# One added wait: an expert's weights are loaded once a scatter has landed

## The reference

```python
scores = softmax(xf @ gate_w.T); topk_w, topk_idx = top_k(scores, 6)      # 64 experts
# each expert takes at most CAP = 128 tokens, in order
buf_tok, buf_w = ...                     # (64, 128): token numbers (T where empty) and weights
gx = xp[buf_tok]                         # gather of 128 rows for each expert
g, u = split(einsum('ech,ehi->eci', gx, gate_up_proj))                    # 512 -> 2 x 192
eo = einsum('eci,eih->ech', silu(g) * u, down_proj) * buf_w[..., None]    # 192 -> 512
routed = zeros.at[buf_tok].add(eo)       # scatter-add
shared = silu(xf @ shared_gate_w.T) * (xf @ shared_up_w.T) @ shared_down_w.T
x = x + routed + shared
```

## Time and profile before

| | us |
|---|---|
| median of 3 runs | 767.88 |
| lowest, highest | 761.12, 768.71 |
| profiled execution, its own time | 772.35 |
| its span in the trace | 770.6 |
| mean granted TensorE clock | 0.903 of full |

### The profile page before, as it was taken

How to read it: one execution, slowest core, us unless ns; L and a number is a source line. 1 busy time by engine, 2 the same in 40 slices (tenths; PEclk the granted TensorE clock), 3 DMA queues, 4 the chain that set the end, 5 groups by cost and what they waited for, 6 DMA issues and landing times.

```text
span 770.6 us, 5725 instructions
## 1 busy us (share of the span) xinstructions
PE 603.0 (78%) x1787; PEld 305.2 (40%) x1787; DVE 304.1 (39%) x724; ACT 144.9 (19%) x298; POOL 223.0 (29%) x191
## 2 busy tenths in 40 slices
PE   5989840498999999988877787897788787977770
PEld 2434320244444444544443344453444443534330
DVE  2987942566679882312212122212122222121120
ACT  4463430244400000111101111111011111110100
POOL 2135664000000003224324334423244433332422
PEclk9999965699999999998998899989898989898995
DMA  9817431731110134798987899878798989888933
GB/s 243 241 56 86 132 111 54 201 110 62 67 58 0 36 132 146 223 279 234 257 227 212 227 270 258 245 219 238 218 273 244 264 244 259 238 242 207 278 48 41
DMA packets 50757, 138.31 MB, mean 179 GB/s; under 512 B 11232, under 2 KB 13920, under 8 KB 50720
## 3 DMA queue, kind: packets, MB, share of 16 engines
q1 hardware_dynamic: 34464, 98.00, 41.2%
q0 software_dynamic: 16256, 39.87, 23.7%
HBM read 107.89 MB, written 29.89 MB: 179 GB/s over the span
## 4 chain that ended last, share of the span: by engine, by line
DMA 50%; PE 16%; issue 7%; DVE 6%; ACT 1%; POOL 0%; POOLq 0%; DVEq 0%; SPq 0%
DMA out<-y,table 50%; PE bank L852 6%; PE bank L864 3%; DVE val L1099 2%; DVE cand L1098 2%; PE bank L832 2%; PE bank L928 2%; PE bank L825 1%; PE bank L916 1%; ACT xnT L948 1%; DVE x L1094 0%; DVE shid L1089 0%; PE bank L908 0%; DMA both<-cand 0%; DVE krep L1070 0%
## 5 line engine op out<-in xcount | busy, mean ns | idle before, releaser
L794 POOL DMA_INDIRECT out<-y,table x64 | 101.6, 1587 | 287.6 <-DMA out<-y,table 259.3
L928 PE MATMUL bank<-gu_w,gxT 128*128 128x384 f32 x512 | 182.4, 501 | 1.2 <-ACT gxT L999 0.8
L1173 DVE TENSOR_SCALAR y<-bank,gx 128x512 f32<-128x512 f32 x64 | 48.1, 751 | 276.9 <-DMA out<-y,table 172.9
L916 PE MATMUL bank<-dn_w,hidT 96*128 96x512 f32 x256 | 145.5, 698 | 1.6 <-DVE hidT L1185 1.6
L928 PEld LDWEIGHTS bank<-gu_w,gxT 128*128 128x128 f32 x512 | 97.0, 200 | 55.6 <-issue 6.4
L800 POOL DMA_INDIRECT gx<-rows_dram,table x64 | 63.5, 992 | 159.1 <-DVE table L1164 139.9
L908 PE MATMUL bank<-ident,gx 128*128 128x128 f32 x256 | 44.9, 303 | 80.9 <-DMA gx<-rows_dram,table 80.9
L852 PE MATMUL bank<-xnT,upT 128*128 128x512 f32 x192 | 84.2, 595 | 0.0
L908 PEld LDWEIGHTS bank<-ident,gx 128*128 128x128 f32 x256 | 32.7, 153 | 109.5 <-DMA gx<-rows_dram,table 98.4
L1007 ACT ACTIVATE eg<-bank 128x192 f32<-128x192 f32 x64 | 21.2, 332 | 283.0 <-PE bank L928 283.0
L916 PEld LDWEIGHTS bank<-dn_w,hidT 96*128 96x128 f32 x256 | 50.7, 219 | 40.8 <-issue 38.3
(11 more groups left out here) (137 smaller groups left out, 456.2 us busy)
## 6 DMA issues: line engine op xcount, KB each, us to landing
gu_w<-in_gate_up SPq DMA_DIRECT2D x64, 768.0 KB, 5.8
dn_w<-in_down SPq DMA_DIRECT2D x64, 384.0 KB, 7.3
rows_dram<-rows SPq DMA_DIRECT2D x4, 1152.0 KB, 4.3
x<-in_x SPq DMA_DIRECT2D x4, 1024.0 KB, 8.5
feat_dram<-feat SPq DMA_DIRECT2D x4, 1024.0 KB, 5.2
out<-x SPq DMA_DIRECT2D x4, 1024.0 KB, 4.4
w<-in_W SPq DMA_DIRECT2D x5, 256.0 KB, 7.3
nodes<-in_ctx SPq DMA_DIRECT2D x4, 256.0 KB, 5.7
```

The lines of the kernel that those rows point to most:

```text
L794: pool.indirect_dma_start(a["out"][:, :], bass.IndirectOffsetOnAxis(ap=table[:, e:e + 1], axis=0), y[:, e % YB, :], None, compute_op=ALU.a ...
L916: last = nc.tensor.matmul(DN[:], hidT[:, e % 2, j, :], dn_w[:, e % U, j, :], start=(j == 0), stop=(j == 1))
L928: last = nc.tensor.matmul(GU[e % 2][:, 0:2 * I], gxT[:, e % 2, c, :], gu_w[:, e % U, c, :], start=(c == 0), stop=(c == KC - 1))
L1173: nc.vector.tensor_scalar(y[:, e % YB, :], DN[:], gx[:, e % GX, D + e:D + e + 1], None, ALU.mult).then_inc(y_ready, 1)
```

## The change

The loop of weight loads on SP's queue gets a second wait. The first (down of e-4 done, the buffer is free) stays. The added one waits until the scatter of expert e-4 has landed. As the diff's loop variable is the expert that is loaded, this is the scatter of expert e for the weights of e+4.

```diff
                 for e in range(U, E):
                     sp.wait_ge(dn_done, e - U + 1)
+                    sp.wait_ge(scat, 16 * (e - U + 1))
                     load_expert(sp, e, e % U)
```

## The result

The changed kernel has a median of 774.97 us over 20 runs (771.42 to 781.94); the kernel before, over its 20 runs, 769.58 (761.12 to 777.50). The ratio is 1.0098, with a 95% interval of 1.007 to 1.0127. I timed the change again in two more series, each beside the kernel before on one chip: 1.0049 (1.002 to 1.0078) and 1.0038 (1.0007 to 1.0068). So it loses 3 to 8 us. I had said 763.7 us, 0.5% less than before. The time lies in the range that I gave (750 to 780) and within the 1% that I called likeliest, but on the other side, and outside the 758 to 771 us of my first case. That case was for intervals of 7.03 to 7.25 us, and the intervals came out in it; what they add up to did not. I had scaled to a median of 767.88 from 3 runs, and 20 runs gave 769.58.

A forecast was written before the change was run, and what follows sets the result against it. The row of scatters, each waiting for the last to land, was taken as the bound. Terms of -6.2, -0.8, -1.8 and +4.6 summed to -4.2 us, giving 763.7 us on the median's scale; range 750 to 780.

The forecast's parts named there:

- my first case: The forecast proper: intervals between scatters of 7.03 to 7.25 us, time 758 to 771 us, chance 0.60.
- The middle: Scatter 5 to 58: 53 intervals at 7.13 us for 7.163, so 1.8 us less.
- four clean pairs: Four ask-and-scatter pairs in the old trace, ask 0.64 to 0.94 us before the scatter's issue; mean interval 7.13 us.
- The start: Scatter 0 to 5: the early burst of loads is spread out; 6.2 us less from scatter 1, 0.8 from scatter 0.
- Scatter 0: First scatter, with no load out: 5.63 us to the next issue for 6.38, so 0.8 us less.
- The end: Scatter 58 to 63: fewer scatters fly without a load beside them; 32.7 us for 28.1, 4.6 more.
- The place of the ask and of the loads: Each load asked for 0.69 us before a scatter's issue, both weights landed 5.97 us after the ask.
- A: Rival, scatters fly longer: ask falls after the issue, interval 7.93 for 7.13, 48 us in all, 812; chance 0.12.
- B: Rival, the load comes on the path: 7.67 us per scatter, +32 us, 796; chance 0.06.
- The slack of 3.2 us: Loop from landing through load, TensorE and VectorE takes 18.2 us for three scatters, where the scatters take 21.4.
- C: Rival, an even stream packs better: 6.9 us per interval, -14 us more, 750; chance 0.22.
- My floor of 6.3 us: The DMA engines' work per interval, taken from a busy share of 0.88; as an interval it would give 714 us.

The follow-up runs named there:

- marked_scatter: The change, but each load waits for a count that GpSimd raises by a memset behind the scatter, not for a landing: 697.94 us, ratio 0.9026.
- before_again: The kernel before the change, with no edit, timed and traced a second time: 771.57 us, ratio 1.0001.

## Why the prediction was wrong

**The middle: 7.13 us for an interval, which measured 7.21.** This is the term that turned the sign. Times 53 it is 4.2 us of the 5.7 us between the predicted -4.2 and the traces' +1.5. The price was the mean of four clean pairs, flight 6.34 plus 0.79. The three traces of the change have flights of 6.36 to 6.41 on average, which is 0.04 more and 2.3 us of the 4.2. My rows held that too: the four scatters landed 7.11 us after their loads' asks on average, with the ask 0.77 before the issue. I used their flight for an ask that I put at 0.69 before; the same landing makes 6.38 at the measured 0.73. The rest, 0.03, is not flight: in every trace of either kernel the interval after scatter 36 holds some 0.9 us in which GpSimd waits for nothing, the one after 52 some 0.3, and in two traces of the change scatter 24 waits for y. I set four pairs without such an event against the 7.163 of the earlier trace rows, which is a mean with the first two in it. A mean should have been compared with a mean: with these two events my pairs give 7.155, and a gain of 0.4 us in place of 1.8. That lucky and unlucky pairs "cancel to the same number" was said without a reason.

**The start: -7.0, measured -4.9.** The direction and the cause are right. Some 0.9 us of the miss is that the trace I read had the slowest start of the three: 34.7 us from scatter 1 to 5, for 33.0 and 33.9. Another 1.0 is that the four intervals took 29.0 to 30.2 us for my 28.5. They are 7.25 to 7.54 us each, longer than in the middle, and no run shows why. Scatter 0 gave 0.5 for the 0.8.

**The end: +4.6, measured +4.1.** Right.

**The place of the ask and of the loads.** I said 0.69 us before the issue; it is 0.73. I said 5.97 us from ask to landed; medians are 0.37 + 5.4 = 5.8. TensorE's wait for each load (some 2 us) is 1.6, the gathers' wait is gone, flights lie nearly all near 6.4. Scatter 5 was issued at 346.8 to 351.5 for my 347. These signs came nearly as written.

**Rivals.** A (flights grow by as much as the ask slips) was priced nearly right, at 7.93 for an ask 0.09 after the issue: 7.95 was measured at 0.14 before and 8.30 at 0.32 after. It did not happen in the change, whose ask does not slip. B (the load on the path) happened once in the first trace, at scatter 24, where SP took 1.23 us over one issue and `dn_w` landed after 6.7: the 5.1 us wait in the fence above. The slack of 3.2 us was nearly right: in the three traces of the change y(e) is done 3.3 us (median) before scatter e is issued, 3.1 with my allowance of 0.25 taken off. At scatter 24 it was 0.3 to 0.75 before that allowance. C (an even stream packs better) did not come from evenness, but it came, at ten per cent, once the even stream was shifted by 2.4 us. My floor of 6.3 us for an interval was no floor. It came from a busy share of 0.88 as if 1.00 were the most, but marked_scatter runs at 6.00 us with a share of 1.04. The packets' time per interval is the same in both, 1.04 x 6.00 and 0.87 x 7.17 (before_again), each 6.2 us: the work did not shrink, the gaps went.

**What stays open.** The traces account for +1.5 us (three each), the series measured +2.9, +3.8 and +7.5 us by their ratios. The first series remains higher than the traces explain.

## What to carry to other kernels

When two transfers share the DMA engines and only one of them is on the path, ask for the other so late that its packets start behind the first one's, and see in the trace that they do. Here that was 1.7 us after the issue; 0.3 us after was worse than before it, and 3.0 us after came too near to the next one. The same load cost 1.5 us per interval ahead of the scatter and 0.3 behind it (7.21 and 6.00 us, for 5.69 with no load). How early a load is asked for matters only until it lands in time. An event of one interval in fifty belongs in a forecast made of clean rows, as it is in the mean that the forecast is compared with; and a gain at the start of a loop is kept only if what caused the burst is gone for good.

## What I had not expected of the hardware

- GpSimd's semaphore instruction ran ahead of the work before it: SP asked 0.14 us before the scatter whose issue the instruction follows in the program, and with a memset of one number in its place 1.70 us after. A memset behind the gather showed as 0.09 us.
- The scatter landed 7.1 to 7.2 us after the ask of the load in three kernels, with the ask from 0.73 us before to 0.32 us after the scatter's own issue. A load's first packet started 0.96 us after its ask, a scatter's 2.16 us after its issue when alone; until the load was through, the scatter's queue moved next to nothing.
- A mean busy share of 1.04 for the DMA engines in marked_scatter, for 0.87 before, at 293 GB/s for 242. A full stretch does not stop at 1.00.
